# Output stage: the variance of a tile by a Square pass on ScalarE instead of two batch-norm statistics on VectorE, the normalising one tile later, and the result in a ring of buffers apart from x

## The reference, cut to what matters

```python
x = x + gnn(layernorm(x), edges, ...)       # two GAT layers, edges plus self loops
x = x + ffn(layernorm(x))                   # 768 -> 96 -> 768, gelu in its tanh form
# layernorm: (x - mean) / sqrt(var + 1e-5), over the 768 features of a node
# ffn: h = x @ W0.T + b0;  h = gelu(h);  out = h @ W1.T + b1
```

## Time and profile before

| | us |
|---|---|
| median of 3 runs | 4296.51 (4296.18 to 4299.38) |
| the profiled execution, its own time | 4294.91 |
| its span, first to last instruction | 4293.2 |
| output stage, first work of VectorE on a tile to the end | 3743 to 4293 |
| of it steady, from tile 8 on (91 tiles) | 3791 to 4271 |

### The profile page before, as it was taken

How to read it: one execution, slowest core, us unless ns; L and a number is a source line. 1 busy time by engine, 2 the same in 40 slices (tenths; PEclk the granted TensorE clock), 3 DMA queues, 4 the chain that set the end, 5 groups by cost and what they waited for, 6 DMA issues and landing times. The chain is left out here.

```text
span 4293.2 us, 67317 instructions
## 1 busy us (share of the span) xinstructions
PE 3523.8 (82%) x21804; PEld 2146.3 (50%) x21805; DVE 2163.2 (50%) x5213; ACT 1302.1 (30%) x2233; POOL 1009.2 (24%) x1392
## 2 busy tenths in 40 slices
PE   4850039999999999999999999999999930188898
PEld 3640025566555655565556555655565520055565
DVE  8877254434443444334434443344334300389998
ACT  2531113322332233223322332233223300044444
POOL 2448710000000000000000000000000037466665
PEclk9985559999999999999999999999999975599999
DMA  8862011111111111111121111111111000278887
GB/s 256 256 211 61 3 38 40 44 56 34 48 40 56 37 46 37 57 38 45 38 56 38 46 40 53 39 48 38 53 39 48 29 13 1 49 213 231 231 230 211
DMA packets 147427, 337.78 MB, mean 79 GB/s; under 512 B 81880, under 2 KB 81880, under 8 KB 139738
## 3 DMA queue, kind: packets, MB, share of 16 engines
q1 hardware_dynamic: 111883, 240.88, 18.4%
q0 software_dynamic: 34112, 93.04, 8.5%
q10 hardware_dynamic: 1175, 0.05, 0.0%
HBM read 266.09 MB, written 124.25 MB: 91 GB/s over the span
## 5 line engine op out<-in xcount | busy, mean ns | idle before, releaser
L942 POOL DMA_INDIRECT lay_rows<-parts,lay_idx x200 | 210.1, 1051 | 2536.2 <-PE lay_pz L1185 1619.2
L1219 PE MATMUL lay_pm<-lay_zh,w1h 128*128 128x500 f16 x1920 | 718.4, 374 | 25.3 <-DVE lay_h L1105 20.1
L1220 PE MATMUL lay_pm<-lay_zl,w1h 128*128 128x500 f16 x1920 | 718.6, 374 | 1.8 <-issue 1.3
L1221 PE MATMUL lay_pm<-lay_zh,w1l 128*128 128x500 f16 x1920 | 718.4, 374 | 0.0
L1026 DVE SCALAR_TENSOR_TENSOR lay_zl<-lay_pz,lay_zh 128x400 f16<-128x400 f32 x600 | 320.4, 574 | 710.7 <-ACT lay_zh L1136 710.5
L1136 ACT ACTIVATE lay_zh<-lay_pz 128x400 f16<-128x400 f32 x600 | 298.3, 504 | 1056.9 <-PE lay_pz L1185 1053.2
L1145 ACT ACTIVATE lay_ex<-lay_pm,b1c,scale 128x500 f32<-128x500 f32 x320 | 245.6, 768 | 869.8 <-PE lay_pm L1221 869.8
L1243 PE MATMUL lay_pm<-w2h,lay_gh 128*128 128x512 f16 x1280 | 484.9, 379 | 0.0
L1243 PE MATMUL lay_pm<-w2h,lay_gl 128*128 128x512 f16 x1280 | 483.9, 378 | 0.0
L1243 PE MATMUL lay_pm<-w2l,lay_gh 128*128 128x512 f16 x1280 | 483.4, 378 | 0.0
L1061 DVE TENSOR_SCALAR lay_ex<-lay_ex,scale 128x500 f32<-128x500 f32 x320 | 153.7, 480 | 568.0 <-ACT lay_ex L1145 568.0
(11 more groups left out here) (278 smaller groups left out, 5775.1 us busy)
## 6 DMA issues: line engine op xcount, KB each, us to landing
x<-in_x_dram SPq DMA_DIRECT2D x20, 1500.0 KB
out_x<-x SPq DMA_DIRECT2D x100, 288.0 KB
out_own<-h SPq DMA_DIRECT2D x100, 288.0 KB
out_dram<-out_x SPq DMA_DIRECT2D x100, 288.0 KB
nrm_xb<-in_x_dram SPq DMA_DIRECT2D x20, 1344.0 KB
parts<-nrm_parts SPq DMA_DIRECT2D x20, 1344.0 KB
h<-lay_h SPq DMA_DIRECT2D x80, 336.0 KB
nrm_w<-in_L_gnn_W_dram SPq DMA_DIRECT2D x6, 1024.0 KB, 19.3
```

The lines of the kernel that those rows point to most:

```text
L1219: pe.matmul(o, c.w1h[:, d, cols], zh[:, d, h], start=(d == 0), stop=False)
L1220: pe.matmul(o, c.w1h[:, d, cols], zl[:, d, h], start=False, stop=False)
L1221: ins = pe.matmul(o, c.w1l[:, d, cols], zh[:, d, h], start=False, stop=(d == DC - 1))
```

## The change

The two statistics and their aggregation leave VectorE. The add of `pa` to `x` becomes one `scalar_tensor_tensor` that also gives the row sums (`total`). Two small operations make of it the negative mean in two scalings (`nm`, `nms`). ScalarE then runs Square over the whole tile with the scaled mean as its bias and with the sum of the squares as its second output (`spread2`), which is the variance. GpSimd adds eps itself, so it has eight small operations in place of seven. `xn` is made one iteration later, and with it all later parts move by one (offsets -1 to -5); there is one iteration more at the end. The last add writes into `result`, a ring of five tiles, and the store reads from there; the load into `x` waits for the last add of the tile that had the slot, not for a store.

```diff
+RB = 5
-        x = m.sb("x", [OT, GT, D])
+        x, result = m.sb("x", [OT, GT, D]), m.sb("result", [OT, RB, D])
-        FIRST, LAST = -AHEAD, TILES + 3
+        FIRST, LAST = -AHEAD, TILES + 4
...
                 if beyond(t, GT):
-                    sp.wait_ge(x_out[at], 32 * there)
+                    sp.wait_ge(o_ready, t + 1 - GT)
...
-                t, at, there, ok = tile_at(grp, j, -4)
+                t, at, there, ok = tile_at(grp, j, -5)
                 if ok:
                     sp.wait_ge(o_ready, t + 1)
...
-                        sp.dma_start(dr.out[bass.ds(OT * t + lo, hi - lo), :], x[lo:hi, at]).then_inc(x_out[at], 16)
+                        sp.dma_start(dr.out[bass.ds(OT * t + lo, hi - lo), :], result[lo:hi, at % RB]).then_inc(out_done[at % RB], 16)
...
-                    pool.wait_ge(ve_ready, t + 1)
+                    pool.wait_ge(dev_ready, t + 1)
+                    nw.link(nc.gpsimd.tensor_tensor(ve_, spread2[:, at % 2:at % 2 + 1], eps[:], ALU.add))
                     nw.link(nc.gpsimd.tensor_tensor(rough_, ve_, power[:], ALU.pow))
...
-                    nc.vector.tensor_tensor(x[:, at], x[:, at], pa[0:OT, 0:D], ALU.add).then_inc(x2_ready, 1)
-                    dve.wait_ge(x2_ready, t + 1)
-                    for half in range(2):
-                        lc.put(nc.vector.bn_stats(stats[:, b, half], x[:, at, half * (D // 2):(half + 1) * (D // 2)]))
-                    lc.wait()
-                    nc.vector.memset(spare[:], 0.0)
-                    lc.link(nc.vector.bn_aggr(mv[:, b], stats[:, b].rearrange("p a b -> p (a b)")))
                     if beyond(t, 2):
                         dve.wait_ge(norm_ready, t - 1)
-                    nc.vector.tensor_scalar(nm[:, col], mv[:, b, 0:1], -1.0, None, ALU.mult)
-                    nc.vector.tensor_scalar(ve[:, col], mv[:, b, 1:2], EPS, None, ALU.add).then_inc(ve_ready, 1)
+                    nc.vector.scalar_tensor_tensor(out=x[:, at], in0=x[:, at], scalar=1.0, in1=pa[0:OT, 0:D], op0=ALU.mult,
+                                                   op1=ALU.add, accum_out=total[:, col]).then_inc(x2_ready, 1)
+                    dve.wait_ge(x2_ready, t + 1)
+                    nc.vector.tensor_scalar(nms[:, col], total[:, col], -1.0 / D ** 1.5, None, ALU.mult)
+                    nc.vector.tensor_scalar(nm[:, col], total[:, col], -1.0 / D, None, ALU.mult).then_inc(mean_ready, 1)
...
                     dve.wait_ge(o_done, tf + 1)
-                    nc.vector.tensor_tensor(x[:, af], x[:, af], po[0:OT, 0:D], ALU.add).then_inc(o_ready, 1)
+                    if beyond(tf, RB):
+                        dve.wait_ge(out_done[af % RB], 32 * (GT // RB * theref + af // RB))
+                    nc.vector.tensor_tensor(result[:, af % RB], x[:, af], po[0:OT, 0:D], ALU.add).then_inc(o_ready, 1)
...
             def iteration(grp, j):
-                tg, ag, _, okg = tile_at(grp, j, -3)
+                t, at, _, ok = tile_at(grp, j, 0)
+                if ok:
+                    act.wait_ge(mean_ready, t + 1)
+                    if beyond(t, 1):
+                        act.wait_ge(dev_ready, t)
+                    if beyond(t, 2):
+                        act.wait_ge(norm_ready, t - 1)
+                    b = at % 2
+                    nc.scalar.activation(dev[:], x[:, at], ACT.Square, bias=nms[:, b:b + 1], scale=D ** -0.5,
+                                         accum_out=spread2[:, b:b + 1]).then_inc(dev_ready, 1)
+                tg, ag, _, okg = tile_at(grp, j, -4)
```

More of the change, by code:

```diff
@@ L1394, in stage_output @@
         att = m.sb("att", [OE, AB, OT])
-        stats, mv = m.sb("stats", [OT, 2, 2, 6]), m.sb("mv", [OT, 2, 2])
+        dev, total, spread2 = m.sb("dev", [OT, D]), m.sb("total", [OT, 2]), m.sb("spread2", [OT, 2])
+        nms, eps = m.sb("nms", [OT, 2]), m.sb("eps", [OT, 1])
         ve, nm, rough, sq, rstd, shift = (m.sb(n, [OT, 2]) for n in ("ve", "nm", "rough", "sq", "rstd", "shift"))
@@ L1415, in stage_output @@
         x_in = [m.sem(f"x_in{j}") for j in range(GT)]
-        x_out = [m.sem(f"x_out{j}") for j in range(GT)]
+        out_done = [m.sem(f"out_done{j}") for j in range(RB)]
         own_in = [m.sem(f"own_in{j}") for j in range(HB)]
@@ L1499, in _ @@
             schedule(sp, iteration)
-            for j in range(GT):
-                sp.wait_ge(x_out[j], 32 * NG)
+            for j in range(RB):
+                sp.wait_ge(out_done[j], 32 * NO // RB)
         @block.gpsimd
@@ L1512, in _ @@
             nc.gpsimd.memset(onehalf[:], 1.5).then_inc(posed, 1)
+            nc.gpsimd.memset(eps[:], EPS).then_inc(posed, 1)
             nc.gpsimd.memset(rows[:], 0.0).then_inc(posed, 1)
-            pool.wait_ge(posed, 4)
+            pool.wait_ge(posed, 5)
             def iteration(grp, j):
@@ L1580, in _ @@
             ch.wait()
-            nc.vector.memset(stats[:], 0.0).then_inc(w_ready, 1)
+            nc.vector.memset(total[:], 0.0).then_inc(w_ready, 1)
             def slot_math(grp):
@@ L1629, in iteration @@
                 col = slice(b, b + 1)
-                lc = Chain(dve, chain, 3 * t)
+                lc = Chain(dve, chain, t)
                 if ok:
@@ L1697, in iteration @@
                     nc.scalar.activation(th[:, ag % 2], u2[:, ag % 2], ACT.Tanh, scale=GELU_C).then_inc(th_ready, 1)
-                t, at, _, ok = tile_at(grp, j, -1)
+                t, at, _, ok = tile_at(grp, j, -2)
                 if ok:
@@ L1705, in iteration @@
                         .then_inc(xt_ready, 1)
-                th_, ah_, _, okh = tile_at(grp, j, -2)
+                th_, ah_, _, okh = tile_at(grp, j, -3)
                 if okh:
@@ L1713, in iteration @@
                     nc.scalar.activation(u2[:, hb], hid[:], ACT.Square, bias=b0s[:], scale=CUBE).then_inc(u_ready, 1)
-                t, at, _, ok = tile_at(grp, j, 0)
+                t, at, _, ok = tile_at(grp, j, -1)
                 if ok:
@@ L1764, in iteration @@
                     ins.then_inc(turned, 1)
-                t, at, _, ok = tile_at(grp, j, -2)
+                t, at, _, ok = tile_at(grp, j, -3)
                 if ok:
@@ L1772, in iteration @@
                     ins.then_inc(h_done, 1)
-                t, at, _, ok = tile_at(grp, j, -3)
+                t, at, _, ok = tile_at(grp, j, -4)
                 if ok:
```

9 lines of the change are left out of this document (4 added, 5 removed).

## The result

The changed kernel takes 4330.95 us in the median of 4 runs (4328.56 to 4339.73), the kernel before 4296.35 us beside it (4289.53 to 4299.38). The ratio is 1.0086, with a 95% interval of 1.0067 to 1.0106. It is slower by 34.6 us. The sign was forecast, and the time lies in the range of 4265 to 4342, but above the forecast's own 4300 to 4325; the sum of the prediction had 13.7 us in place of 34.6.

What follows compares the result with a forecast made beforehand. VectorE was taken as the bound (steady tile 4.79 us, mean 5.27), TensorE close behind. 91 tiles x 0.14 us = 12.7, +1 at the end, on 4294.91 gave 4308.6, stated as 4309; range 4265 to 4342.

Steps and rivals of the forecast that it cites:

- VectorE is freed and does not set the time: On VectorE, 1.15 us of 4.79 a tile go, so it could do a tile in 3.65.
- Square stands behind `xn`, 4.50 us after its sum: On ScalarE, Square waits for `xn` and the `hid` readings, starting 4.50 us after its tile's sum begins, ending at 5.6.
- slower by more: Rival: all ten tiles at 5.58 us plus half the late-gather cost, 5.8 us a tile, +48 us, 4345; chance 0.12.
- Square costs 1.1 us: On ScalarE, the added pass over 100x768 takes 1.02 us, plus 0.1 for the sum output.
- The ring 0 and the end about nothing: Result buffers and loads without store waits: 0, between -0.1 and +0.1 us a tile; one more iteration at the end: +1 us.
- The late stretches, 0.48 us a tile: Some gathers in each group of ten land late, lifting the tile from the steady 4.79 us to the mean 5.27.
- GpSimd's free turn of 4.50: GpSimd's unhindered time from gather to gather, 4.23 us now plus 0.27 for one more dependent operation.
- Then GpSimd is late and becomes the bound: GpSimd's small operations wait beside VectorE's own-row add, one hit losing 0.75 to 1.2 us on top of 4.50.
- 5.6 that "keeps itself up": At a GpSimd turn of 4.50 + 1.1 us the own-row add again falls among the multiplies, until a gather lands late.
- The collisions: VectorE's two-operand own-row add holds GpSimd's small operations, among the multiplies; six tiles in ten at 5.58 us.
- The loop at 4.69, with late landings 5.13: Sum, Square, GpSimd, gather three tiles on, landing: (8.95 + 5.13) / 3 = 4.69 us a tile, plus 0.44 for late landings.
- a rival for "faster": Own-row add nearly always falls behind GpSimd's small operations, loss 0: 5.13 us a tile, -13 us, 4283; chance 0.20.

Runs made afterwards that it cites:

- The run with Square ahead: The changed kernel with ScalarE's Square of tile t+1 put before `xn` of tile t-1 instead of behind it; 4298.54 us, 1.0020 of the kernel before.
- The one without any collision: The changed kernel with VectorE's add of the own rows reading one SBUF operand (`x1` left out, output not the reference's); 4303.63 us, 1.0030 of the kernel before.

## Why the prediction was right and where it was wrong

The kernel got slower, as forecast, but not for the reason that the sum gave; the sign is right partly by luck. Term by term:

**VectorE is freed and does not set the time:** right. Busy 336 us in place of 454, with waits for `pa`.

**Square stands behind `xn`, 4.50 us after its sum:** right where TensorE runs at 2.4 GHz (4.43). It is 6.14 where the clock had fallen, and that case was given only to the rival "slower by more".

**Square costs 1.1 us:** right, 0.93 and 0.19 for the accumulator. **The ring 0 and the end about nothing:** right, the ring by a run of its own, and both within 1.0003 in the run with the later order and the ring.

**The late stretches, 0.48 us a tile:** a wrong reading, which did not decide. The difference between the steady tile of 4.79 and the mean of 5.27 was put down to late gathers. But VectorE waited 1.2 us for `pa` in 480; it was busy 454 / 91 = 4.99 us a tile, since it has the extra work for the next group (its masks, line 1593, alone take 15.9 us), and waited 9.4 us for own rows. This is why the earlier gather gained nothing on the kernel before.

**GpSimd's free turn of 4.50:** too long. It is 4211.96 - 4207.75 = 4.21, as much as before with one operation less: the first operation now starts at once behind the gather (0.03 us, not 0.17), and the last gap before the next gather is shorter (0.63 us, not 0.72).

**"Then GpSimd is late and becomes the bound", with 1.1 us lost in a turn, and 5.6 that "keeps itself up":** this is the step that failed: GpSimd's turn was made the bound. The loss is 0.38 us on the small operations and 0.065 on the gather, together 0.45, and was 0.46 before. (By waits it comes out the same: (480 - 78.2 - 5.2) / 85 = 4.67 us are GpSimd's own, less 4.21.) Its wait did not go from 0.72 to under 0.3 but to 0.92. The collisions did come where they were forecast, among the multiplies: over half a microsecond is lost in 41 of 78 turns, 0.86 us in the mean of these (1.1 in six of ten had been forecast). But GpSimd then waits for Square, so its turn is not what sets the time.

The run with Square ahead restored three quarters of the loss with the collisions in place. The one without any collision restored two thirds and left GpSimd waiting longer. The two overlap, since both shorten the same way from sum to gather, and neither stands for the loss alone. The Trainium skill's rule ("SBUF — State Buffer", section "SBUF: two separate sides"), by which a VectorE operation with two SBUF inputs and a GpSimd operation that reads SBUF exclude each other, agrees with the trace here: beside 1.01 us of add a 0.19 us operation takes 1.03 to 1.05. The loss of 0.46 us a turn was there before as well, although the prediction also says that hardly anything was lost, and cost nothing that shows while VectorE was the bound and GpSimd waited 0.72 us a tile for it. In the changed kernel it lies on the way that sets the time.

**The loop at 4.69, with late landings 5.13:** right as a mechanism and the one that decides, but too short, 5.59 being the mean; with 5.13 the prediction had it as a rival for "faster". Both legs were too short. From gather to sum 5.13 was used, read from a sum that had not waited for its rows, and with the landing counted from the end of the gather's instruction. Counted from its start, as the trace has it, the best landing takes 3.8 us and the mean one 5.7, for 19 of 75 take over 7 us and the row had shown one buffer of ten. The landed rows then stand another 1.0 us in the mean until TensorE comes to them, which makes 6.71. This leg was as long before (6.85). From sum to gather 8.95 was for a tile with nothing in its way. The shortest pieces of the trace give 4.43 (Square after its sum) + 1.11 (to GpSimd's first operation) + 3.09 (to the gather) = 8.63, and the mean of 10.06 has 0.31 more in the first, 0.63 in the second and 0.49 in the third. The first is Square delayed behind `hid` and `xn`, for which the stretch above shows the low clock after a late landing; on this way it is at most 0.31 / 3 = 0.10 us a tile. The other two go with the collisions, and all but 0.16 + 0.17 of them are gone with the one-operand add.

So the prediction had seen that the work taken from VectorE comes back as time behind `xn`, but it got its slowdown from GpSimd's turn, and its own loop would have given 13 us in the other direction. That the sign came out is in part luck: the 5.6 us of a turn that was not the bound stood beside the 5.59 of a loop that was. How much of the first 0.31 us is the clock was not measured; no run held the clock.

## What to carry to other kernels

When work moves from a full engine to an idle one, ask where in the idle engine's order it stands and whose results come before it there: 1.1 us of work on an engine with more than half its time free put 2.10 us into the way from sum to gather and took 1.33 out, because it stood behind a reading that came late. Then draw the loop that the result closes, divide it by the tiles it spans, and compare it with the engine's time before moving anything, with the mean of a landing and not its best; if the loop is the longer, give it another tile first. A change that loses alone can win with its partner: here 1.0086 became 0.9958 by one constant.

## What the runs showed of the hardware that was not expected

- A VectorE pass over 100x768 with a single operand in SBUF closed nothing to GpSimd: in 89 such passes of 1.01 us the small operations kept means of 196 to 203 ns (`pow`, 579 ns, is as long as ever).
- The gather's own instruction is lengthened beside a two-operand add too: 1.45 us in one case, 1277 ns in the mean, both with Square ahead, and 1081 and 1085 ns with the one-operand add.
- Reading the accumulator takes 0.19 us on ScalarE and 0.08 on VectorE, and the next instruction on ScalarE starts 0.1 us after that reading starts.
- A buffer whose store was issued shortly before its next load cost 185 us of waits in 480, where the same store two turns ahead had cost 34.4.
- The time to land of one gather form spreads from 3.8 to over 9 us in one stage, and over 7 us in 19 of 75 both before and after the change, mostly at the fifth to eighth tile of a group. Why there was not tested.
